# First up product of a mixture-of-experts stage without its second gather, last ranks between its halves, and the list of the 18 later tiles finished ahead of the first gated tile

## The chip, the cores and the metric

The kernel runs on one core of one Trainium2 chip. The metric is the device time of one execution in microseconds; the profiled execution has a span a little below its own time, since the span counts from the first to the last recorded instruction. Engines are named as in the profile: PE is TensorE, PEld its weight load, DVE is VectorE, ACT is ScalarE, POOL is GpSimd, SP is the engine that issues most transfers. A "q" behind an engine's name is its queue (its sequencer).

## The reference

Two layers over x of shape (2, 512, 128), all in float32: cross attention to 77 context rows with 16 heads, then a feed-forward stage of 8 experts of which each row takes the best two. The second layer is what the change touches.

```python
def _L0_ffn_ref(x, Wg, bg, W1, b1, W3, b3, W2, b2):
    logits = x @ Wg + bg
    probs = softmax(logits)
    top_v, top_i = top_k(probs, 2)
    top_v = top_v / (top_v.sum(-1, keepdims=True) + 1e-06)
    combine = einsum('bsk,bske->bse', top_v, one_hot(top_i, 8))
    out = zeros_like(x)
    for e in range(8):
        h = silu(x @ W1[e] + b1[e]) * (x @ W3[e] + b3[e])
        out = out + combine[..., e:e + 1] * (h @ W2[e] + b2[e])
    return out

x = x + _L0_xattn_ref(_layernorm(x), ctx_1024, ...)
x = x + _L0_ffn_ref(_layernorm(x), ...)
```

## The kernel before

The 1024 rows stand in 8 row tiles of 128 (`T = 8`), in three groups: tiles 0 to 3, 4 and 5, 6 and 7. Every row goes to two experts, so there are 2048 pairs of row and expert. They are sorted by expert into `NT = 23` expert tiles of 128 slots, each with the rows of one expert only. The first `FULL = 5` expert tiles are filled from the pairs of groups 0 and 1, before the last row tiles have left the attention; the other 18 take what is left.

The sort is arithmetic on VectorE and TensorE. For a group, `top_two` finds the two experts of each row and writes `sel`; `count_ranks` on TensorE multiplies `sel` by triangular matrices, which gives every pair its rank within its expert; `ranks` and `blocks_of` on VectorE read that out. `first_tiles` and `other_tiles` turn ranks into a list (`hit_1` for 5 tiles, `tile_hit` for 18) that says which pair stands in which tile, `one_hots` writes the permutation `perm` within a tile, and `slot_rows` on TensorE multiplies both (12 or 16 narrow products), so that the row number of every slot comes out in PSUM. VectorE writes them to `idx` (`other_rows` for the 18), and `other_experts` writes the experts' numbers to `eid`.

The expert stage runs over the tiles j = 0 to 22. GpSimd gathers the 128 rows of a tile from memory (`gather`, an indirect transfer), eight tiles ahead, and later scatters the result (`scatter`). TensorE transposes them (`expert_xT`, L1224), ScalarE copies the transpose out of PSUM (L650), TensorE forms the two up products (`up`, L1237: the gate half with W1, the linear half with W3; 16 matrix instructions a tile), ScalarE applies Silu to the gate half (L661), VectorE multiplies (`gated`, L970), TensorE forms the down product (`down`, L1248) and VectorE adds its bias (`bias_down`, L979). The weights of four tiles lie ready (`WR = 4`); SP loads those of tile j when the linear half of tile j - 4 is done. An expert's number is read from `eid` into a register (`value_load`) by each engine that needs it.

Each engine runs its instructions in the order in which they are written. An instruction that waits for a semaphore holds up all behind it on its engine. So the order on TensorE, VectorE and GpSimd around the start of the expert stage is written out by hand, and the change moves things in it. On TensorE it was:

```python
count_ranks(2); expert_xT(0); expert_xT(1)
up(0); expert_xT(2)
up(1); expert_xT(3); slot_rows(T * K, tile_hit, ...); down(0)
up(2); expert_xT(4); down(1)
...
```

On VectorE, behind `other_tiles`: `gated(0)`, `one_hots(2)`, `other_experts`, `gated(1)`, `other_rows`, `bias_down(0)`, `gated(2)`, and so on. On GpSimd: gathers 0 and 1, `rstd_step(6)` (the root of the variance of row tiles 6 and 7, which `top_two(2)` and `normed(2)` need), gathers 2 to 7. Gather 0 waits for the `idx` of the first 5 tiles, gather 5 for that of the 18 and for the last rows in memory.

Of the kernel before, what the change touches and what calls it, by code (L numbers as in the profile page):

```python
# [33 lines left out]
def build(nc, x, ctx_in, w_q, w_kv, w_out, gamma, beta, w_g, b_g, w_1, b_1, w_3, b_3, w_2, b_2, out):  # L34
# [18 lines left out]
    with ctx:  # L53
# [368 lines left out]
        def _(pool):  # L422
# [93 lines left out]

            AHEAD = 8
            for j in range(AHEAD):
                if j == 2:
                    rstd_step(4 + G - 1)  # L520
                gather(j)
            for j in range(NT):
# [152 lines left out]
        def _(dve):  # L675
# [210 lines left out]
            def other_tiles():  # L886

                link(dve.tensor_copy(floor_2[:, PAIRS_1:T * K], floors[:, PAIRS_1:T * K]))
                link(dve.scalar_tensor_tensor(out=padded[:, :], in0=TOTALS[1], scalar=ROUND_128, in1=taken_r[:, :],
                                              op0=ALU.add, op1=ALU.subtract))  # L890
                link(dve.tensor_tensor(low_pad[:, :, 0:E], lower[:, :, :], over_pairs(padded[:, :], E), ALU.mult))
                link(dve.tensor_reduce(base[:, :], low_pad[:, :, :], AX.X, ALU.add))
                link(dve.tensor_tensor(based[:, :, :, :].rearrange("p t k e -> p (t k) e"), masks, over_pairs(base[:, :], T * K), ALU.mult))
                link(dve.tensor_reduce(start_of[:, :, :], based[:, :, :, :], AX.X, ALU.add))
                starts = start_of[:, :, :].rearrange("p t k -> p (t k)")
                link(dve.tensor_tensor(starts, starts, floor_2[:, :], ALU.add))
                link(dve.tensor_tensor(tile_hit[:, :, :],
                                       iota_j[:, FULL:NT].rearrange("p (o j) -> p o j", o=1).broadcast_to([P, T * K, NT - FULL]),
                                       starts.rearrange("p (n o) -> p n o", o=1).broadcast_to([P, T * K, NT - FULL]),
                                       ALU.is_equal))  # L900
                dve.tensor_tensor(tile_hit[:, :, :], tile_hit[:, :, :],
                                  vals.rearrange("p (n o) -> p n o", o=1).broadcast_to([P, T * K, NT - FULL]),
                                  ALU.mult).then_inc(hit_ok, 1)
# [48 lines left out]
            ranks(2)  # L952
            blocks_of(2)
            other_tiles()

            dve.wait_ge(eid_1_ok, 1)
            dve.wait_ge(ld["bias"], 16)
# [16 lines left out]
            def bias_down(j):  # L974

                dve.wait_ge(y_mm, j + 1)
                if j >= YR:
                    dve.wait_ge(y_st[j % YR], 16 * (j // YR))
                dve.tensor_tensor(y_sb[:, j % YR, :], Y_AT[j % 2],  # L979
                                  b2[:, bass.ds(expert[j], 1), :].rearrange("p e d -> p (e d)"), ALU.add).then_inc(y_ok, 1)  # L980
# [10 lines left out]
            for j in range(NT + 1):  # L991
                if j < NT:
                    gated(j)
                if j == 0:
                    one_hots(2)
                if j >= 1 and j != 1:
                    bias_down(j - 1)
                if j == 0:
                    other_experts()
                elif j == 1:  # L1000
                    other_rows()
                    bias_down(0)
                elif j == FULL:
                    dve.tensor_tensor(shifted[:, :, :], top_v[:, :, :], top_v[:, :, 0:1].broadcast_to([P, T, E]),
                                      ALU.subtract).then_inc(shift_ok, 1)

# [11 lines left out]
        def _(pe):  # L1018
# [204 lines left out]
                    pe.wait_ge(xt_ok, j)  # L1223
                pe.transpose(psum[:, 6, 0:P], xg[:, j % GR, :], ident[:, :]).then_inc(xt_mm, 1)  # L1224

            def up(j):

                if j == FULL:
                    pe.wait_ge(eid_ok, 1)
                expert[j] = pe.value_load(eid[0:1, j:j + 1], min_val=0, max_val=E - 1)  # L1230
                pe.wait_ge(xt_ok, j + 1)
                pe.wait_ge(w_ok[j % WR], 32 * (j // WR + 1))
                for a, (freed, done) in enumerate(((silu_ok, gate_mm), (h_ok, lin_mm))):
                    if j >= 2:
                        pe.wait_ge(freed, FC * (j - 1))
                    for c in range(FC):
                        ins = pe.matmul(psum[:, 2 * (j % 2) + a, c * P:(c + 1) * P],  # L1237
                                        w13[:, j % WR, a, c * P:(c + 1) * P],
                                        xt[:, j % XR, :], start=True, stop=True)
                    ins.then_inc(done, 1)  # L1240

            def down(j):

# [74 lines left out]
            slot_rows(FIRST * K, hit_1, FIRST_AT, hit_1_ok, idx_1_mm)  # L1318
            tokens_x2T(2)
            logits(2)  # L1320
            count_ranks(2)
            pe.wait_ge(ld["experts"], 16 * E)
            pe.wait_ge(eid_1_ok, 1)
            expert_xT(0)
            expert_xT(1)
            for j in range(NT + 1):
                if j < NT:
                    up(j)
                if j + 2 < NT:
                    expert_xT(j + 2)  # L1330
                if j == 1:
                    slot_rows(T * K, tile_hit, OTHER_AT, hit_ok, idx_mm)
                if j >= 1:
                    down(j - 1)


# [25 lines left out]
```

## Time and profile before

| what | value |
|---|---|
| three runs, us | 166.34, 167.34, 168.57 (median 167.34) |
| the profiled execution, its own time, us | 168.23 |
| span of the profiled execution, us | 166.2 |
| TensorE busy (matmul) | 135.3 us, 81% of the span |
| VectorE busy | 107.1 us, 64% |
| ScalarE busy | 76.6 us, 46% |
| GpSimd busy | 78.9 us, 47% |
| mean granted clock of TensorE | 0.934 of full |

Times in the profile's views are microseconds from the span's start. A busy share is a mean over stages with different limits: the attention fills the first 70 us or so, the routing of the last rows follows, and the expert stage fills 83 to 152 us. A granted clock of 1.00 is 2.4 GHz, 0.50 is 1.2 GHz.

### The profile page before, as it was taken

The page shows a single profiled execution, that of the slowest core. Times are in us where ns is not written, and L with a number is a line of the kernel's source. Part 1 is how long each engine was busy: PE and PEld are TensorE (multiplying, and loading weights), DVE is VectorE, ACT ScalarE, POOL GpSimd, SP SyncE. Part 2 cuts the span into 40 slices and gives each one's busy share as a digit, 9 for nine tenths or more (in the row PEclk, how much of TensorE's full clock was granted, in tenths as well). Part 3 has the DMA queues.
Part 4 walks back from the last instruction along what each step waited for, and adds up shares of the span by engine and source line. Part 5 has one row for each costly group of instructions (what it writes and reads, how often), then busy time and mean ns, then how long its engine had stood idle before and what let it go on. Part 6 is the DMA issues. An engine that isn't in the chain of part 4 may idle for free.

```text
span 166.2 us, 3861 instructions
## 1 busy us (share of the span) xinstructions
PE 135.3 (81%) x1109; PEld 127.1 (76%) x1109; DVE 107.1 (64%) x345; ACT 76.6 (46%) x210; POOL 78.9 (47%) x98
## 2 busy tenths in 40 slices
PE   6499697889999999864299889999999999994000
PEld 6398586669988999863199789999999999994000
DVE  0685899998899968986758626363636363535074
ACT  3048565875564698600333523545454444444000
POOL 2760300956553685106700677777777744244000
PEclk9999999999999999996569999999999999999555
DMA  4999700011000002338704776877788775300453
GB/s 143 287 319 279 220 2 0 0 63 67 0 2 4 0 0 62 101 111 284 266 21 132 213 243 194 206 262 226 235 248 261 223 264 191 115 16 32 137 165 95
DMA packets 21629, 23.63 MB, mean 142 GB/s; under 512 B 2349, under 2 KB 14473, under 8 KB 21609
## 3 DMA queue, kind: packets, MB, share of 16 engines
q1 hardware_dynamic: 19300, 19.51, 38.3%
q0 software_dynamic: 1472, 3.02, 6.1%
q10 hardware_dynamic: 837, 0.87, 1.5%
q8 instruction: 9, 0.15, 0.4%
q14 instruction: 11, 0.09, 0.2%
HBM read 19.98 MB, written 3.41 MB: 141 GB/s over the span
## 4 chain that ended last, share of the span: by engine, by line
PE 63%; DVE 13%; DMA 10%; ACT 6%; issue 3%; POOL 1%; SPq 1%; ACTq 0%; POOLq 0%; DVEq 0%
PE psum L1237 25%; PE psum L1248 11%; PE psum L1282 8%; PE psum L1264 5%; DMA early<-in_L_xattn_W_kv_dram 4%; DMA g_room<-xf_scratch,idx 3%; PE psum L1021 2%; PE psum L1023 2%; PE psum L1089 2%; PE psum L1022 2%; DMA y_back<-y_scratch 2%; PE psum L1224 2%; DVE prob L747 2%; DVE xn L1014 2%; DVE negmax L742 2%
## 5 line engine op out<-in xcount | busy, mean ns | idle before, releaser
L1237 PE MATMUL psum<-probT,w 128*128 128x128 f32 x368 | 46.5, 281 | 0.7 <-ACT probT L650 0.7
L970 DVE SCALAR_TENSOR_TENSOR probT<-psum,bias_col,prob 128x128 f32<-128x128 f32 x92 | 26.0, 344 | 31.5 <-ACT prob L661 28.9
L1237 PEld LDWEIGHTS psum<-probT,w 128*128 128x128 f32 x368 | 44.4, 197 | 1.3 <-ACT probT L650 0.9
L661 ACT ACTIVATE prob<-psum,bias_col 128x128 f32<-128x128 f32 x92 | 26.3, 369 | 35.6 <-PE psum L1237 33.4
L505 POOL DMA_INDIRECT g_room<-xf_scratch,idx x23 | 22.7, 987 | 23.7 <-DVE idx L917 8.8
L480 POOL TENSOR_TENSOR prob<-prob,rowsum 128x1232 f32<-128x1232 f32 x8 | 18.0, 2251 | 15.3 <-DVE rowsum L738 15.3
L514 POOL DMA_INDIRECT y_scratch<-xnT,out_row x18 | 17.6, 980 | 14.9 <-DVE xnT L979 11.9
L1248 PE MATMUL psum<-w,probT 128*128 x184 | 24.4, 276 | 0.0
L1248 PEld LDWEIGHTS psum<-w,probT 128*128 128x128 f32 x184 | 22.3, 192 | 0.1
L1282 PE MATMUL psum<-vo,probT 128*128 128x128 f32 (+1 forms) x160 | 19.3, 276 | 0.0
L1282 PEld LDWEIGHTS psum<-vo,probT 128*128 128x128 f32 (+1 forms) x160 | 18.5, 192 | 0.0
L601 ACT ACTIVATE probT<-psum 128x512 f32<-128x512 f32 (+1 forms) x24 | 10.9, 493 | 7.5 <-PE psum L1264 7.5
L742 DVE TENSOR_REDUCE negmax<-psum 128x16 f32<-128x1232 f32 x8 | 11.5, 1433 | 2.2 <-PE psum L1023 2.2
L747 DVE TENSOR_TENSOR prob<-psum,negmax 128x1232 f32<-128x1232 f32 x8 | 11.5, 1441 | 0.3
L1264 PE MATMUL psum<-ident,prob 128*128 128x128 f32 x80 | 11.3, 276 | 0.4 <-ACT vo L601 0.4
L735 DVE TENSOR_REDUCE rowsum<-prob 128x16 f32<-128x1232 f32 x8 | 11.3, 1418 | 0.3 <-ACT prob L584 0.3
L584 ACT ACTIVATE prob<-prob 128x1232 f32<-128x1232 f32 x8 | 9.8, 1228 | 2.9 <-DVE prob L747 2.9
L1021 PE MATMUL psum<-g_room,xn_hi 128*128 128x512 f32 (+1 forms) x24 | 9.1, 379 | 1.3 <-issue 1.3
L1264 PEld LDWEIGHTS psum<-ident,prob 128*128 128x128 f32 x80 | 8.7, 140 | 1.2 <-issue 0.6
L1023 PE MATMUL psum<-g_room,xn_hi 128*128 128x512 f32 (+1 forms) x24 | 8.5, 355 | 0.0
L1022 PE MATMUL psum<-g_room,xn_lo 128*128 128x512 f32 (+1 forms) x24 | 8.5, 355 | 0.0
L460 POOL TENSOR_SCALAR rstd<-mv 128x4 f32<-128x4 f32 (+1 forms) x7 | 1.9, 264 | 13.7 <-DVE mv L694 13.7
(162 smaller groups left out, 185.7 us busy)
## 6 DMA issues: line engine op xcount, KB each, us to landing
w<-in_L_ffn_W_dram SPq DMA_DIRECT2D x54, 256.0 KB, 4.8
early<-in_L_xattn_W_kv_dram SPq DMA_DIRECT2D x2, 512.0 KB, 7.5
y_back<-y_scratch SPq DMA_DIRECT2D x4, 256.0 KB, 3.5
early<-in_L_xattn_W_q_dram ACTq DMA_DIRECT2D x1, 512.0 KB, 8.3
early<-in_L_xattn_W_out_dram SPq DMA_DIRECT2D x1, 512.0 KB, 10.1
early<-in_L_ffn_b_dram SPq DMA_DIRECT2D x1, 512.0 KB, 4.3
xf_scratch<-xf SPq DMA_DIRECT2D x2, 256.0 KB, 2.6
xf_scratch<-xf SPq DMA_DIRECT2D x4, 128.0 KB, 2.2
```

The source lines that it names most:

```text
L480: pool.tensor_tensor(prob[:, t % NP_, :].rearrange("p (h m) -> p h m", h=H), prob[:, t % NP_, :].rearrange("p (h m) -> p h m", h=H), rowsu ...
L505: pool.indirect_dma_start(xg[:, j % GR, :], None, xf_dram[:, :], bass.IndirectOffsetOnAxis(ap=idx[:, j:j + 1], axis=0)).then_inc(xg_ok[j % ...
L514: pool.indirect_dma_start(y_dram[:, :], bass.IndirectOffsetOnAxis(ap=rows_of[:, j:j + 1], axis=0), y_sb[:, j % YR, :], None).then_inc(y_st ...
L661: act.activation(silu[:, j % 2, c, :], psum[:, 2 * (j % 2), c * P:(c + 1) * P], ACT.Silu, bias=bias_col[:, 0, bass.ds(expert, 1), c]).then ...
L742: dve.tensor_reduce(negmax[:, t, :], scores(t), AX.X, ALU.max, negate=True).then_inc(s_dve, 1)
L747: dve.tensor_tensor(heads(t), scores(t), negmax[:, t, :].rearrange("p (h o) -> p h o", o=1).broadcast_to([P, H, M]), ALU.add).then_inc(s_s ...
L970: dve.scalar_tensor_tensor(out=hT[:, j % 2, c, :], in0=psum[:, 2 * (j % 2) + 1, c * P:(c + 1) * P], scalar=bias_col[:, 1, bass.ds(expert[j ...
L1021: pe.matmul(dst, w_h, m_h, start=True, stop=False)
L1237: ins = pe.matmul(psum[:, 2 * (j % 2) + a, c * P:(c + 1) * P], w13[:, j % WR, a, c * P:(c + 1) * P], xt[:, j % XR, :], start=True, stop=True)
L1248: ins = pe.matmul(Y_AT[j % 2], hT[:, j % 2, c, :], w2[:, bass.ds(expert[j], 1), c, :].rearrange("p e d -> p (e d)"), start=(c == 0), stop= ...
L1264: ins = pe.transpose(bank[0:rows(c), k * P:(k + 1) * P], prob[:, t % NP_, c * P:c * P + rows(c)], ident[:, :])
L1282: ins = pe.matmul(bank[:, 0:P], probT[0:rows(c), t % 2, c, :], vo[0:rows(c), t // TB, c, :], start=(c == 0), stop=(c == CH - 1))
```

## The change

GpSimd does `rstd_step(6)` ahead of gather 1 instead of ahead of gather 2. TensorE starts `up(0)` after `expert_xT(0)` alone; `count_ranks(2)` goes between the gate half and the linear half of `up(0)`; then come `expert_xT(1)`, `expert_xT(2)` and the `slot_rows` of the 18 tiles, and only then `up(1)`. VectorE does `one_hots(2)` and `other_experts` ahead of `gated(0)` instead of behind it, and `other_rows` behind `gated(0)` instead of behind `gated(1)`.

```diff
             AHEAD = 8
             for j in range(AHEAD):
-                if j == 2:
+                if j == 1:
                     rstd_step(4 + G - 1)
                 gather(j)
...
             other_tiles()
+            one_hots(2)
+            other_experts()
...
                 if j < NT:
                     gated(j)
                 if j == 0:
-                    one_hots(2)
-                if j >= 1 and j != 1:
+                    other_rows()
+                else:
                     bias_down(j - 1)
-                if j == 0:
-                    other_experts()
-                elif j == 1:
-                    other_rows()
-                    bias_down(0)
-                elif j == FULL:
+                if j == FULL:
                     dve.tensor_tensor(shifted[:, :, :], ...)
...
-            def up(j):
+            def up(j, between=None):
...
                     ins.then_inc(done, 1)
+                    if a == 0 and between is not None:
+                        between()
...
             logits(2)
-            count_ranks(2)
             pe.wait_ge(ld["experts"], 16 * E)
             pe.wait_ge(eid_1_ok, 1)
             expert_xT(0)
+            up(0, lambda: count_ranks(2))
             expert_xT(1)
-            for j in range(NT + 1):
+            expert_xT(2)
+            slot_rows(T * K, tile_hit, OTHER_AT, hit_ok, idx_mm)
+            for j in range(1, NT + 1):
                 if j < NT:
                     up(j)
                 if j + 2 < NT:
                     expert_xT(j + 2)
-                if j == 1:
-                    slot_rows(T * K, tile_hit, OTHER_AT, hit_ok, idx_mm)
-                if j >= 1:
-                    down(j - 1)
+                down(j - 1)
```

## Rows read from the trace of the kernel before

**Rows 1.** The chain that ended last, 60 to 167 us: start, length, what.
```profile
77.23 4.69 DMA g_room<-xf_scratch,idx
81.92 0.12 issue
...
83.15 3.47 PE psum L1237 x16
...
102.43 0.89 PE psum L1248 x8
103.32 1.79 PE psum L1237 x16
105.11 0.11 PE psum L1224
```

**Rows 2.** Order of time, 66 to 101 us; in brackets the idle time before, and what ended it.
```profile
72.52 5.56 SPq L387 DMA_DIRECT2D w<-in_L_ffn_W_dram  x8
...
75.69 1.24 POOL L505 DMA_INDIRECT g_room<-xf_scratch,idx  x1 [8.62 <-DVE idx L947]
...
78.21 0.26 POOL L460 TENSOR_SCALAR rstd<-mv 128x2 f32<-128x2 f32 x1
...
79.38 0.16 DVE L778 SCALAR_TENSOR_TENSOR shift<-mv,rstd 128x2 f32<-128x2 f32 x1 [1.49 <-POOL rstd L462]
...
80.77 0.17 DVE L799 TENSOR_TENSOR sel<-mask 128x16 f16<-128x16 f32 x1
...
81.00 0.20 PE L1200 MATMUL psum<-sel,ones 128*128 128x24 f16 x1 [3.27 <-DVE sel L799]
...
81.31 0.19 DVE L806 TENSOR_TENSOR ranked<-mask,psum 128x32 f32<-128x32 f32 x1 [0.36 <-PE psum L1202]
...
82.04 0.45 PE L1224 MATMUL psum<-ident,g_room 128*128 128x128 f32 x1 [0.46 <-DMA g_room<-xf_scratch,idx]
...
84.62 0.46 DVE L901 TENSOR_TENSOR tile_hit<-tile_hit,val 128x288 f16<-128x288 f16 x1
...
86.57 1.95 PE L1237 MATMUL psum<-probT,w 128*128 128x128 f32 x16
...
87.84 0.68 DVE L827 TENSOR_TENSOR perm<-iota_q,q_of 128x512 f16<-128x512 f16 x1
...
88.47 0.55 PE L1213 MATMUL psum<-tile_hit,perm 128*128 128x18 f16 x16
...
89.46 0.16 DVE L912 TENSOR_SCALAR eid<-eid_f 1x18 int32<-1x18 f32 x1
...
90.31 1.13 DVE L970 SCALAR_TENSOR_TENSOR probT<-psum,bias_col,prob 128x128 f32<-128x128 f32 x4 [0.69 <-issue]
...
91.36 0.23 DVE L917 TENSOR_SCALAR idx<-psum,row_base 128x18 uint32<-128x18 f32 x1
...
91.86 0.95 POOL L505 DMA_INDIRECT g_room<-xf_scratch,idx  x1 [8.78 <-DVE idx L917]
...
96.09 0.33 PE L1224 MATMUL psum<-ident,g_room 128*128 128x128 f32 x1 [1.28 <-DVE probT L970]
...
100.37 1.95 PE L1237 MATMUL psum<-probT,w 128*128 128x128 f32 x16
```

**Rows 3.** Gathers (L505): gather 0 alone, then those from 69 to 99 us.
```profile
DMA to landing us min/median/max: 4.5/4.5/4.5
...
DMA to landing us min/median/max: 2.8/4.2/4.7
```

**Rows 4.** L1230 (the expert's number into a register), TensorE's queue, 71 to 100 us.
```profile
L1230 PEldq TENSOR_LOAD <-eid x6: 297/308/612, 82.1 to 98.4; - x6
```

**Rows 5.** Stretches: length, busy time (instructions) by engine, granted clock, transfers' share, GB/s.
```profile
73.20:75.90 2.70, 0.63 (x14) 0.57 (x14) 2.43 (x12) 0.00 (x0) 0.21 (x1) 1.00 0.73 221
76.00:81.00 5.00, 1.17 (x6) 0.93 (x4) 3.06 (x20) 1.26 (x3) 4.08 (x6) 0.50 0.85 308
83.10:86.20 3.10, 3.05 (x14) 3.08 (x15) 1.81 (x6) 0.86 (x4) 0.00 (x0) 0.50 0.10 28
86.20:88.90 2.70, 2.70 (x39) 2.69 (x37) 2.04 (x8) 1.70 (x8) 0.00 (x0) 1.00 0.18 23
```

**Rows 6.** Transfers of the page, by line: transfers, KB each, median us to landing.
```profile
w<-in_L_ffn_W_dram SPq DMA_DIRECT2D x54, 256.0 KB, 4.8
```

## The prediction

> **What bounds the kernel now.** I read the chain of waits first, then the order of time around the diff, then the clock. From about 97 us to 149 us the chain is TensorE without a gap: a tile of the expert stage is 0.89 us of down product, 1.79 us of up product and 0.11 us of transpose, so 2.79 us a tile, repeated unchanged [rows 1]. Nothing in the diff touches that stretch or the tail behind it. So the question is only when TensorE enters it: I take the start of `up(5)`, 100.37 us before [rows 2], as the mark, and whatever moves it moves the end.
>
> Ahead of the mark four things cost time. (1) TensorE stands 3.27 us in front of `count_ranks(2)`, waiting for `sel` [rows 2]. Gather 0 had landed by then: issued at 75.69 [rows 2], 4.5 us to landing [rows 3], so 80.2. (2) It then waits for gather 1 until 82.04 [rows 1, 2], and `up(0)` starts at 83.15. (3) `up(0)` takes 3.47 us against 1.79 us later [rows 1], because the granted clock is 0.50 (1.2 GHz) from about 76 to 86.2 and 1.00 (2.4 GHz) afterwards [rows 5]. (4) Before `expert_xT(5)` it stands 1.28 us, since gather 5 goes out only at 91.86, after `idx` at 91.36 [rows 2]. The change attacks (1), (2) and (4).
>
> **Part 1, `rstd_step(6)` ahead of gather 1.** On POOL the step took from 78.21 to `shift` at 79.38, 1.17 us, and VectorE stood 1.49 us for it [rows 2]. Gather 0's instruction ends at 76.93, so the step now starts there, `shift` falls at 78.1 and `sel` (1.56 us later, 79.38 to 80.94 [rows 2]) is ready at 79.7 instead of 80.94. Gather 1 starts at about 78.2 instead of 77.23; by its own 4.69 us [rows 1] it lands at 82.9. Gathers 2 to 4 keep their places, as the step stood ahead of gather 2 before. `normed(2)` and SP's two stores of the last rows move 1.2 us forward; only gather 5 waits for them, and it waits longer for `idx`. Taken alone the step is worth nothing here, because of part 2: `sel` is now asked for only at 83.1.
>
> **Part 2, `up(0)` without gather 1, ranks between its halves.** `expert_xT(0)` at 80.3 (landing plus 0.12, as after gather 1 [rows 1]). From a transpose to the first product of `up(0)` went 1.11 us (82.04 to 83.15 [rows 1, 2]), in which TensorE's queue reads the expert's number (a register load, 0.61 us the first time [rows 4]) and ScalarE copies; so `up(0)` starts at 81.4, 1.7 us sooner. Its weights were issued from 72.52 [rows 2] and land in a median of 4.8 us [rows 6]; they are there. The gate half costs half of 3.47, 1.73 us, to 83.15; then the four small rank products, which VectorE reads 0.31 us after they begin (81.00 to 81.31 [rows 2]): `ranks(2)` at 83.45, against 81.31 before. **This is the price of the change: the list for the 18 tiles starts 2.1 us later.** The linear half ends at about 85.0, transposes 1 and 2 at about 86.3 with the copy between them (gather 1 landed at 82.9 and is hidden; if it took all of the margin to 85.0 it would begin to cost).
>
> **Part 3, what is now queued behind the list.** `slot_rows` of the 18 tiles stands ahead of `up(1)` on TensorE. `ranks(2)` to the end of `tile_hit` took 81.31 to 85.08, 3.77 us; the permutation, moved in front of `gated(0)`, 0.68 us [rows 2]: 83.45 + 3.77 + 0.68 = 87.9. Until then TensorE can do 12 of the 16 slot products and no more; `up(1)`, whose rows and weights are ready since 86, waits behind them, and all that follows. After 87.9 come the last 4 slot products (a quarter of 0.55 us [rows 2]) and the register load of `up(1)`, which is no longer hidden. No row shows this pair; bounds: 0.2 us (load hidden) and 1.25 us (0.14 plus the 1.11 us in front of `up(0)`). I take 1.05, near the upper one, because the queue holds at the same kind of wait as there, with nothing behind it. So `up(1)` starts at 88.95 instead of 86.57 [rows 2], **2.4 us later**.
>
> On VectorE, `other_experts` now stands ahead of `gated(0)`: 1.1 us (88.52 to 89.62 [rows 2]), then 0.69 us of register load [rows 2]: `gated(0)` at about 89.7, done by 90.9. Who waits: `down(0)`, due at 88.95 + 1.79 + 0.11 = 90.85. Four pieces follow one another at VectorE's pace of 0.28 us, so it hardly stops, but the load for `up(2)` is again behind that wait: 0 to 0.6 us, taken as 0.3. ScalarE's first Silu products come after its second copy, before 88, well ahead of `gated(0)`.
>
> **Part 4, what is given back.** From `up(1)` on no list stands between the tiles. `up(1)` to `up(5)` is then 4 x 2.79 = 11.2 us; before it was 86.57 to 100.37, 13.8 us, with the slot products and the 1.28 us. `other_rows` stands behind `gated(0)` instead of `gated(1)`: `idx` 1.05 us after its start (90.31 to 91.36 [rows 2]), so 90.75, gather 5 0.5 us later at 91.25, landing some 4.2 us after that at 95.5. It is wanted at 96.3 or later: hidden, by 0.8 us; without that cover each late microsecond counts. The weights of tile 5 wait for `up(1)` (90.75 instead of 88.5), land 4.8 us [rows 6] and an issue later, some 96.5, and are wanted at 100.
>
> **Sum.** `up(5)` at 88.95 + 11.16 + 0.3 = 100.4, against 100.37. The wait for gathers is exchanged for a wait for the list, one for one: **0.0 us, from -1.1 to +0.7** by the bounds named.
>
> **The clock.** That sum counts TensorE at 2.4 GHz from `up(1)` on. Before, TensorE was busy 0.63 of the 2.70 us from 73.2 to 75.9, 12 narrow slot products and two transposes in the main, and the clock then fell; it came back at 86.2, at the end of 3.05 us of dense work [rows 5]. The change makes a second thin stretch of the same kind: from 86.3 to 88.95 there are 16 narrow slot products, 0.55 us, and it comes right when the clock has just risen. If it is at 1.2 GHz when `up(1)` begins, that product costs 3.47 instead of 1.79 us [rows 1]: at most 1.7 us more; if it falls or rises inside the product, less. I take 1.2 us.
>
> The Trainium skill (TensorE: Matmul & The Clock Gate, section Loop structure matters more than you think) warns of the same thing: a wait between matmuls lets the engine go cold, and the next ones run slow. Its section on the PE-mode transpose says that transposes do not count as busy work in the same way, so the two of part 2 would not help to hold the clock. By this rule the time is the higher one; by a clock that stays up, the sum stands at 0.0.
>
> **Scale.** The profiled execution took 168.23 us; the three runs have the median 167.34, 0.89 below it. I put each difference on the median. The profiled one lies inside their spread (166.34 to 168.57); if its surplus was a low clock under `up(0)`, which the new order does not shorten, the runs after may lie up to 0.9 us higher.
>
> **Rivals.** *Forecast, 0.45:* the exchange is even and the low clock takes some of `up(1)`: 167.34 + 0.0 + 1.2 = 168.5, from 167.9 to 170.0. *Clock stays up, 0.30:* for it, dense work from 81.4 to 85.0 is as long as what raised it before; against it, the thin stretch: 167.3, from 166.5 to 168.0. *The list is hidden, 0.16:* if the gate half runs at 2.4 GHz it takes 0.87 us less and the list follows at once: 166.5; if the list were ready when the transposes are, `up(1)` could start at 86.9 and `up(5)` at 98.1, 2.3 us earlier: 165.0. For it: the clock's fall at 75.9 came late in a thin stretch and need not come in each run. Against: that list has 1.6 us to make up, and in the trace none of its 14 steps has slack. *Slower, 0.09:* the clock does not come back after `up(1)`, because the wait for `gated(0)` breaks the dense work again. A whole tile at 1.2 GHz costs 2.79 us more, and through `up(2)` it is 2.79 + 1.7 = 4.5: 171.8. It decides from the point where the low clock lasts beyond `down(0)`. Against it: before, the clock rose under one product. *That it does not do what it says* would be gather 0 landing later than 80.2; the rows give 2.8 to 4.7 us for one [rows 3], so 0.2 us at most; it is inside the bounds.
>
> **The numbers.** About 2% (3.3 us) is what a measurement of this kernel can tell from no change. Faster by more needs below 164.0, under even the hidden list's 165.0: 0.04. Slower needs above 170.7: the slow rival, 0.09. Within: 0.87. The range for 8 in 10 goes from 166.2 (most of the hidden list left out) to 170.2 (the forecast's end with the surplus).
>
> **What would show it.** `up(0)` near 81.4, `ranks(2)` near 83.5, TensorE idle some 2 us in front of the slot products, ended by VectorE's `tile_hit` and `perm`; `up(1)` near 89 and its length (1.8 or 3.5 us) with the granted clock; no wait in front of `expert_xT(5)`; `up(5)` at 100 to 102. The prediction is wrong if `slot_rows` finds its list ready, if gather 5 still ends a wait, or if `down(0)` stands for `gated(0)` by more than half a microsecond.

## The result, and the profile after

| | before | changed |
|---|---|---|
| median of 4 runs each, us | 167.95 | 170.64 |
| lowest and highest, us | 166.34, 169.36 | 168.71, 171.53 |
| ratio, 95% interval | | 1.0145 [1.0086, 1.0203] |
| profiled execution: own time, span, us | 168.23, 166.2 | 171.53, 169.5 |
| mean granted clock | 0.934 | 0.912 |

The changed kernel is slower by 1.45%, some 2.4 us. The ratio leaves out executions more than 1.5% above the fastest of their kernel, the profiled one of the changed kernel among them, so it is not the quotient of the two medians. The forecast of 168.5 and its range to 170.2 were too low.

The two profiles first have to be laid over each other. Gather 0 is issued at 75.69 us before [rows 2] and at 76.62 after, although the change does nothing ahead of it; across the profiles below that issue lies anywhere between 74.2 and 76.7. So all times of the stage are given here **from gather 0's issue**. From there to the end of the span went 90.5 us before (166.2 - 75.69) and 92.9 after (169.5 - 76.62): 2.4 us, the same as the timed ratio.

The chain of waits of the changed kernel (start, length, what), as in [rows 1]; in the new line numbers L1221 is the transpose, L1234 the up product, L1247 the down product, L1210 the slot products:

```profile
76.62 4.18 DMA g_room<-xf_scratch,idx
...
82.25 2.05 PE psum L1234 x8
84.42 0.20 DVE ranked L806
...
87.74 0.46 DVE tile_hit L901
88.19 0.61 DVE perm L827
88.86 0.27 PE psum L1210 x4
89.13 0.54 issue
89.66 3.75 PE psum L1234 x16
93.41 0.21 PE psum L1221
93.63 1.71 PE psum L1247 x8
95.33 1.81 PE psum L1234 x16
```

What stands here is the path that the prediction laid out: the gate half of `up(0)` alone, `ranked`, the steps of the list, `perm`, the last four slot products, the register load ("issue"), `up(1)`. New are the two lengths behind it. `up(1)` takes 3.75 us, and `down(0)` 1.71, where a down product takes 0.89 in [rows 1].

The order of time of the same run (start, length, engine, line, operation; in brackets the idle time before it), for the lines that answer to [rows 2]:

```profile
79.11 0.16 DVE L778 SCALAR_TENSOR_TENSOR shift<-mv,rstd 128x2 f32<-128x2 f32 x1 [0.29 <-POOL rstd L462]
...
80.50 0.17 DVE L799 TENSOR_TENSOR sel<-mask 128x16 f16<-128x16 f32 x1
...
84.42 0.19 DVE L806 TENSOR_TENSOR ranked<-mask,psum 128x32 f32<-128x32 f32 x1 [3.75 <-PE psum L1199]
...
88.25 0.88 PE L1210 MATMUL psum<-tile_hit,perm 128*128 128x18 f16 x16 [0.83 <-DVE tile_hit L901]
...
91.97 0.23 DVE L917 TENSOR_SCALAR idx<-psum,row_base 128x18 uint32<-128x18 f32 x1
...
92.47 0.95 POOL L505 DMA_INDIRECT g_room<-xf_scratch,idx  x1 [8.41 <-DVE idx L917]
...
103.56 1.61 PE L1234 MATMUL psum<-probT,w 128*128 128x128 f32 x13
```

VectorE stood 3.75 us in front of `ranked`, for the rank products that now run in the middle of `up(0)`; its `sel` was done at 80.7. The last line is `up(5)`, the mark. It stands 26.94 us behind gather 0, against 24.68 before: 2.26 us of the 2.4. Behind the mark nothing differs by more than 0.1 us.

The stretches (length, busy time with instructions of PE, PEld, DVE, ACT, POOL, then the granted clock, the transfers' share, GB/s), to be read against [rows 5]:

```profile
78.40:82.20 3.80, 0.45 (x1) 0.18 (x1) 1.76 (x14) 1.16 (x3) 2.99 (x4) 0.50 0.97 331
82.20:86.50 4.30, 4.25 (x21) 3.83 (x21) 1.76 (x10) 0.00 (x0) 1.55 (x2) 0.50 0.29 84
86.50:89.60 3.10, 1.22 (x18) 0.76 (x17) 2.86 (x10) 1.59 (x6) 0.00 (x0) 0.50 0.41 135
89.60:95.10 5.50, 5.44 (x25) 5.47 (x26) 2.98 (x13) 1.42 (x5) 2.02 (x3) 0.50 0.11 34
95.50:99.00 3.50, 3.50 (x34) 3.50 (x34) 1.59 (x6) 1.31 (x5) 2.59 (x4) 1.00 0.62 203
```

Here is where the time went. The clock falls to 1.2 GHz ahead of `up(0)`, as before. Then 4.25 us of nearly dense work in `up(0)` do not bring it back, a thin stretch follows (1.22 us busy of 3.10), and `up(1)` and `down(0)` run through at 1.2 GHz. It fell at 78.2 and is back at 2.4 GHz only at 95.3; before, it fell at 75.9 and was back at 86.2. Run 7 below, the same order on TensorE in an execution of 170.67 us, shows the same lengths: `up(1)` 3.75 us, and 5.46 us from `up(1)` to `up(2)`, where this profile has 5.47.

### The profile page after: what moved, and what is told of

The parts are those of the page before. It is cut to its first block, busy times and chain, and to the rows that moved or that the text cites. A ratio compares the mean times of both kernels' runs of the same rounds, so it can differ in the third digit from the quotient of the medians.

```text
span 169.5 us, 3861 instructions
## 1 busy us (share of the span) xinstructions
PE 138.8 (82%) x1109; PEld 130.6 (77%) x1109; DVE 107.1 (63%) x345; ACT 76.6 (45%) x210; POOL 78.8 (47%) x98
## 4 chain that ended last, share of the span: by engine, by line
PE 64%; DVE 15%; DMA 9%; ACT 4%; issue 3%; POOL 1%; SPq 1%; ACTq 0%; POOLq 0%; DVEq 0%
PE psum L1234 25%; PE psum L1247 12%; PE psum L1281 8%; PE psum L1263 5%; DMA early<-in_L_xattn_W_kv_dram 4%; PE psum L1086 3%; DMA g_room<-xf_scratch,idx 2%; PE psum L1018 2%; PE psum L1020 2%; PE psum L1019 2%; DMA y_back<-y_scratch 2%; DVE prob L747 2%; DVE xn L1011 2%; DVE negmax L742 2%; PE psum L1221 2%
## 5 line engine op out<-in xcount | busy, mean ns | idle before, releaser
L1234 PE MATMUL psum<-probT,w 128*128 128x128 f32 x368 | 48.8, 289 | 1.4 <-ACT probT L650 0.9
L1234 PEld LDWEIGHTS psum<-probT,w 128*128 128x128 f32 x368 | 46.4, 204 | 1.7 <-ACT probT L650 1.1
L505 POOL DMA_INDIRECT g_room<-xf_scratch,idx x23 | 22.7, 985 | 23.3 <-DVE idx L947 8.6
L1247 PE MATMUL psum<-w,probT 128*128 x184 | 25.1, 282 | 0.0
L1247 PEld LDWEIGHTS psum<-w,probT 128*128 128x128 f32 x184 | 23.2, 198 | 0.1
L1018 PE MATMUL psum<-g_room,xn_hi 128*128 128x512 f32 (+1 forms) x24 | 9.1, 379 | 1.3 <-issue 1.3
L650 ACT ACTIVATE probT<-psum 128x128 f32<-128x128 f32 x23 | 6.7, 292 | 6.8 <-PE psum L1221 6.8
L1221 PE MATMUL psum<-ident,g_room 128*128 128x128 f32 x23 | 6.9, 301 | 3.2 <-DMA g_room<-xf_scratch,idx 2.7
```

The source lines that it names most:

```text
L505: pool.indirect_dma_start(xg[:, j % GR, :], None, xf_dram[:, :], bass.IndirectOffsetOnAxis(ap=idx[:, j:j + 1], axis=0)).then_inc(xg_ok[j % ...
L1018: pe.matmul(dst, w_h, m_h, start=True, stop=False)
L1247: ins = pe.matmul(Y_AT[j % 2], hT[:, j % 2, c, :], w2[:, bass.ds(expert[j], 1), c, :].rearrange("p e d -> p (e d)"), start=(c == 0), stop= ...
```

## The experiments

What is to be told apart: is the loss (a) the clock, (b) the wait for the list in front of `up(1)`, or (c) something else in the new order, such as the early `rstd_step`? Two tools serve for it. The first is filling: products of the identity with itself, put where TensorE stands idle and written to a place of PSUM that is written anew before it is read, to hold the clock up (`hold(n)` is n products, each two matrix instructions; ten took 2.48 us in run 1). The second moves `slot_rows` and the ranks. No kernel leaves any of the computation out. "Mark" is the start of `up(5)` in the profiled run, from gather 0. One execution of each run was profiled, and the granted clock differs between executions, so marks and times agree only loosely. In the changed orders `up(0)` starts anywhere from 5.46 to 6.05 us, as gather 0 lands, so a mark alone is good to about half a microsecond.

**1. The changed kernel with filling ahead of `up(0)` and five products in front of the last `slot_rows`.**

```diff
+            def hold(n):
+                for k in range(n):
+                    pe.matmul(psum[:, 2, 0:P], ident[:, :], ident[:, :], start=True, stop=True)
...
+            hold(5)
             slot_rows(FIRST * K, hit_1, FIRST_AT, hit_1_ok, idx_1_mm)
+            hold(2)
             tokens_x2T(2)
+            hold(2)
             logits(2)
+            hold(10)
...
+            hold(5)
             slot_rows(T * K, tile_hit, OTHER_AT, hit_ok, idx_mm)
```

> The changed order, with extra products of the identity on TensorE in its idle stretches (5 before the first slot products, 2 and 2 around the transposes of the last rows, 10 behind the logits, 5 before the slot products of the 18 tiles); they write a free PSUM bank and nothing reads them. Theory A (the order is an even exchange and the loss is the low clock through up(1) and down(0)): the granted clock stays at 1.00, the gate half takes 0.9 us instead of 2.05, the list starts 1 us sooner, up(1) takes 1.8 us; up(5) starts some 23.3 us after gather 0 is issued instead of 26.9, so about 3.5 us below the changed kernel, 1.2 us below the kernel before. Theory B (the loss is the wait for the list in front of up(1), whatever the clock): the time stays within 1 us of the changed kernel, about 2 us over the kernel before.

Measured: 166.86 us, ratio to before 0.9969 [0.9933, 1.0005], against 1.0145 without the filling. Mark 24.91, 2.03 less. Products that compute nothing take away some 1.8% of the time: the clock it is, in the main. But one part was not cured. The stretches of this run, and `up(1)` from its order of time:

```profile
83.00:84.10 1.10, 1.10 (x11) 0.93 (x9) 0.96 (x5) 0.93 (x4) 0.00 (x0) 1.00 0.16 28
84.10:86.40 2.30, 0.75 (x18) 0.57 (x17) 2.16 (x7) 0.38 (x2) 0.00 (x0) 1.00 0.60 216
86.90:90.00 3.10, 3.10 (x17) 3.10 (x16) 1.59 (x7) 1.14 (x4) 0.77 (x1) 0.50 0.01 3
```
```profile
86.39 3.57 PE L1234 MATMUL psum<-probT,w 128*128 128x128 f32 x16 [0.52 <-issue]
```

`up(0)` ran at full clock (1.13 and 1.14 us a half). After the wait for the list (0.75 us busy of 2.30) the clock fell, 0.2 us into `up(1)` (at 86.6). So the clock can be lost in this wait also where it stood at 2.4 GHz.

**2. The kernel before with the same filling ahead of `up(0)`** (`hold(12)` behind `logits(2)`).

```diff
             logits(2)
+            hold(12)
             count_ranks(2)
```

> The order before, with the same extra products of the identity (5, 2, 2, and 12 behind the logits). Theory A: up(0) takes 1.8 instead of 3.5 us and the mark comes 1.5 us sooner: 1 to 1.7 us below the kernel before, and equal to the changed order with held clock within 0.5 us. Theory B: gather 5 ends the wait in front of up(4) anyway, so no change from the kernel before (within 0.5 us), and the changed order with held clock stays 2 us above it.

Measured: 167.16 us, 0.9965 [0.9917, 1.0013], mark 24.53 (before 24.68). In the profiled run the filling ended at 79.7, the clock fell at about 82.9, just as `up(0)` began, and `up(0)` took 3.65 us. The filling was too short, so this run doesn't tell what the order before costs at full clock; run 9 does.

**3. The slot products behind `up(1)`, as before, everything else changed.**

```diff
-            slot_rows(T * K, tile_hit, OTHER_AT, hit_ok, idx_mm)
             for j in range(1, NT + 1):
                 if j < NT:
                     up(j)
                 if j + 2 < NT:
                     expert_xT(j + 2)
+                if j == 1:
+                    slot_rows(T * K, tile_hit, OTHER_AT, hit_ok, idx_mm)
                 down(j - 1)
```

> The change with one part undone: the slot products of the 18 tiles stand behind up(1) and its transpose again, as before; all else as changed. Theory A: TensorE goes from up(0) through two transposes to up(1) with hardly a gap, so the clock is back before up(1) ends; down(0) waits for gated(0) behind the list; up(5) some 24.5 us after gather 0: about 2.4 us below the changed kernel, level with the kernel before (within 0.7 us). Theory B: the wait for the list moves to down(0) and costs the same: within 0.7 us of the changed kernel.

Measured: 168.47 us, 1.0059 [1.0013, 1.0105], mark 25.29, 1.65 less than changed. `up(1)` now waits for no list and starts at 11.49 instead of 13.04, yet it takes 3.73 us. The wait is worth 1.5 us at `up(1)`, and taking it away alone doesn't bring the clock back in time.

**4. Run 3 with the filling of run 1 ahead of `up(0)`, and `other_experts` moved behind `other_rows`.**

```diff
             one_hots(2)
-            other_experts()
...
                 if j == 0:
                     other_rows()
+                    other_experts()
```

> A candidate: the change with the slot products behind up(1), other_experts behind gated(0) and other_rows on VectorE, and the extra products of the identity ahead of up(0) as in the first run. Theory A: clock at 1.00 throughout; list ready about 87, hidden by up(1); up(5) some 21.5 us after gather 0, 3 us below the kernel before (164.5 to 166). Theory B: the wait for the list is the cost and it is hidden here, so also below the kernel before, but no lower than the run without extra products.

Measured: 165.0 us, 0.987 [0.9755, 0.9985], mark 22.48. With no wait for the list and the clock up, `up(1)` starts at 9.17 and takes 2.02 us. Both causes taken away give a kernel faster than before.

**5. Run 1 with the wait for the list filled as well.**

```diff
-            hold(5)
+            hold(8)
             slot_rows(T * K, tile_hit, OTHER_AT, hit_ok, idx_mm)
+            hold(2)
...
+                    if k == 0 and t == FIRST:
+                        hold(2)
                     if k == 0 and t in (0, FIRST):
```

> The changed order with the identity products ahead of up(0) as before (5, 2, 2, 10), and more of them in the second thin stretch: 8 ahead of the slot products of the 18 tiles, 2 between the first 12 and the last 4, 2 behind them. Theory A (the low clock through up(1) is the whole loss): up(1) takes 1.8 instead of 3.6 us, up(5) stands some 23.3 us behind the issue of gather 0; about 1.5 us below the first held run, so 165.3. Theory B (the wait for the list is the loss): no change from the first held run, 166.9.

Measured: 167.43 us, 0.9969 [0.9932, 1.0005], as run 1. Mark 24.24. The stretch in front of `up(1)` and `up(1)` itself, then both up products in the order of time:

```profile
85.70:89.10 3.40, 3.19 (x40) 2.99 (x40) 3.12 (x11) 1.31 (x5) 0.00 (x0) 1.00 0.44 154
89.10:91.10 2.00, 2.00 (x20) 2.00 (x20) 0.94 (x5) 0.76 (x3) 0.00 (x0) 1.00 0.03 12
```
```profile
89.15 1.95 PE L1236 MATMUL psum<-probT,w 128*128 128x128 f32 x16
...
92.41 2.02 PE L1236 MATMUL psum<-probT,w 128*128 128x128 f32 x16 [0.30 <-issue]
```

The clock is now 1.00 throughout and `up(1)` takes 1.95 us, 1.6 less than in run 1. At the mark only 0.67 of it is left and in the time nothing: `up(1)` starts 0.49 later than in run 1 (0.41 of it already at `up(0)`), and from `up(1)` to `up(2)` go 3.26 us instead of 2.79, because `down(0)` now comes before `gated(0)` is done and the register load for `up(2)` stands behind that wait. This is the bubble of the prediction, 0.47 us (it took 0.3); at 1.2 GHz the slow `up(1)` had hidden it.

**6. Run 1 with transposes as the filling**, two for each product.

```diff
-                    pe.matmul(psum[:, 2, 0:P], ident[:, :], ident[:, :], start=True, stop=True)
+                    pe.transpose(psum[:, 2, 0:P], ident[:, :], ident[:, :])
+                    pe.transpose(psum[:, 2, 0:P], ident[:, :], ident[:, :])
```

> The first held run with each extra product replaced by two transposes of the identity, equally long on TensorE. If transposes hold the clock as products do: same as the first held run (166.9, clock 1.00 ahead of up(0)). If they don't count: the clock falls near 78 us as in the changed kernel and the time is about that of the changed kernel (170).

Measured: 167.84 us, 0.9999 [0.9962, 1.0036], mark 23.97. Stretches of its profile:

```profile
77.50:82.00 4.50, 3.09 (x25) 2.69 (x25) 2.43 (x16) 1.16 (x3) 3.57 (x6) 1.00 1.00 341
...
88.60:90.60 2.00, 1.95 (x17) 1.98 (x18) 0.94 (x5) 0.68 (x3) 0.00 (x0) 1.00 0.02 9
```

Here the clock stays at 1.00 with transposes: from 77.5 through `up(1)`, where the changed kernel's stood at 0.50 from 78.4. Two transposes fill as long as one product: ahead of `up(0)` 2.37 us against 2.48 in run 1, in front of the slot products 1.25 against 1.28. That run 1 lost the clock in this wait and run 6 didn't, with all but the same busy time, need not be due to the kind of filling; one profile of each can't tell. The time is no better than run 1's.

**7. `rstd_step` back in its old place, the rest changed.**

```diff
-                if j == 1:
+                if j == 2:
                     rstd_step(4 + G - 1)
```

> The change with one part undone: rstd_step(6) behind gather 1 again. Both theories: sel comes 1.2 us later, still 2 us before count_ranks(2) asks for it, so the same time as the changed kernel within 0.5 us (ratio to before 1.012 to 1.018). If it is lower, the late gather 1 did cost; if higher, sel was asked for sooner than the trace shows.

Measured: 170.84 us, 1.0164 [1.0089, 1.0239], mark 27.40; changed 1.0145 and 26.94. Part 1 makes no difference that can be told in this order, as predicted. The stretches of this run show something else:

```profile
81.00:84.00 3.00, 2.93 (x16) 2.89 (x17) 0.65 (x4) 0.00 (x0) 1.22 (x2) 0.50 0.49 133
84.30:87.60 3.30, 1.31 (x18) 0.81 (x17) 3.02 (x11) 1.59 (x6) 0.00 (x0) 1.00 0.31 91
88.40:93.90 5.50, 5.44 (x25) 5.47 (x26) 3.01 (x13) 1.42 (x5) 2.00 (x3) 0.50 0.06 15
```

In this run `up(0)` did raise the clock (its second half took 1.67 us instead of 2.06), and it was lost again: it fell at about 87.7, before `up(1)`, which took 3.75 us as ever. So the low `up(1)` doesn't hang on whether `up(0)` raises the clock.

**8. Run 4 without its filling** (the list late, the clock left alone).

```diff
-            hold(10)
```

(and the other `hold` lines likewise)

> The candidate without extra products: slot products behind up(1), other_experts behind gated(0) and other_rows. Theory A: up(0) and up(1) follow each other closely, the clock is low under up(0) and most of up(1) as in the third run, but VectorE reaches gated(0) 1.1 us sooner: 1 us below the third run, so 167.5, level with the kernel before; the candidate with held clock stays 2.5 us below it. Theory B: the list is hidden, so level with the candidate with held clock (165).

Measured: 168.82 us, 1.0022 [0.9966, 1.0078], mark 25.94; 167.5 had been expected. Without filling `up(1)` starts at 11.32 and takes 3.76 us. The filling ahead of `up(0)` is worth 3.46 us at the mark in this order (25.94 - 22.48), and some 2.5 us by the two ratios.

**9. The kernel before at full clock**: run 2 with filling around its transposes.

```diff
+            hold(2)
             expert_xT(0)
+            hold(3)
             expert_xT(1)
+            hold(3)
             for j in range(NT + 1):
```

> The order before with identity products in all its idle stretches up to up(0) (5, 2, 2, 12, and 2, 3, 3 around the first two transposes), so that up(0) itself runs at 2.4 GHz. Theory A (at equal clock the two orders are an even exchange): up(5) some 24.2 us behind the issue of gather 0, as in the changed order at full clock (24.24), 0.4 us below the kernel before. Theory C (the even sum had the low clock under up(0) in it, and at equal clock the changed order is the slower one): up(0) takes 1.8 instead of 3.5 us and everything behind it, idx and gather 5 too, comes 1.5 us sooner: up(5) at 23.2, 1.5 us below the kernel before and 1 us below the changed order at full clock.

Measured: 165.93 us, 0.99 [0.9859, 0.9941], mark 23.38. From its order of time, `up(0)`, `up(1)` and the transpose of tile 5:

```profile
82.54 2.02 PE L1237 MATMUL psum<-probT,w 128*128 128x128 f32 x16
84.50 1.95 PE L1237 MATMUL psum<-probT,w 128*128 128x128 f32 x16
...
93.98 0.33 PE L1224 MATMUL psum<-ident,g_room 128*128 128x128 f32 x1 [1.06 <-DVE probT L970]
```

So the kernel before paid for the clock too, 1.3 us at the mark, and at full clock it still has the wait for gather 5 (issued at 90.01, landed 3.9 us later), 1.06 us, that the change removes.

**10. The changed kernel with only the wait for the list filled.**

```diff
+            hold(3)
             slot_rows(T * K, tile_hit, OTHER_AT, hit_ok, idx_mm)
```

> The changed order with identity products in its second thin stretch alone (3 ahead of the slot products of the 18 tiles, 1.3 us at 1.2 GHz); the clock has fallen near 78 us as without them. Theory A: with them the work from up(0) on is dense enough for the clock to come back about the start of up(1): up(1) 1.8 to 2.5 us instead of 3.75, 1.5 us below the changed kernel (ratio to before about 1.005). If the first thin stretch (74 to 81 us) is what counts: no change from the changed kernel (1.0145).

Measured: 168.59 us, 1.008 [1.0035, 1.0126], mark 24.65, 2.29 less than changed. Its stretches, then the filling (L1260) and `up(1)`:

```profile
81.00:85.20 4.20, 3.99 (x21) 3.52 (x20) 1.96 (x11) 0.18 (x1) 1.39 (x2) 0.50 0.34 97
85.40:88.10 2.70, 1.69 (x23) 1.37 (x24) 2.49 (x9) 1.30 (x5) 0.00 (x0) 1.00 0.54 171
```
```profile
85.58 0.83 PE L1260 MATMUL psum<-ident 128*128 128x128 f32 x6
88.10 2.02 PE L1234 MATMUL psum<-probT,w 128*128 128x128 f32 x16 [0.52 <-issue]
```

`up(0)` is at 1.2 GHz throughout (2.05 and 2.06 us a half). The clock is back at 85.4, before the first product of the filling at 85.58, so the filling didn't raise it. What differs from run 7, where the clock also came back with `up(0)`, is that it lasts: it stays at 1.00 through the wait, and `up(1)` takes 2.02 us. So this profile shows the changed order with the clock lost under `up(0)` alone. That the three products kept it is likely from run 7, but rests on one profile of each. The time moves by less than the mark (0.65% or 1.1 us), and the mean clocks of its ten executions go from 0.909 to 0.948, so the clock may not be caught in each.

**11. Part 1 alone in the kernel before.**

```diff
             for j in range(AHEAD):
-                if j == 2:
+                if j == 1:
                     rstd_step(4 + G - 1)
```

> The kernel before with rstd_step(6) ahead of gather 1 and nothing else. Both theories: sel comes 1.2 us sooner, but gather 1 lands 1 us later and up(0) still waits for it: up(0) at 84.1 instead of 83.15; list 1.2 us sooner, gated(0) and idx 1 us later; 0.5 to 1.0 us over the kernel before (ratio 1.003 to 1.006), within what can be told from no change.

Measured: 167.67 us, 0.9992 [0.9947, 1.0036]. `up(0)` starts 0.56 us later (8.02 instead of 7.46), since it still waits for gather 1; the mark is at 24.40 against 24.68. A loss of 0.3 to 0.6% was expected; there is none that can be told.

**12. Run 4 with `other_experts` later still**, behind `gated(1)` and the `bias_down` of tile 0.

```diff
                     other_rows()
-                    other_experts()
                 else:
                     bias_down(j - 1)
+                if j == 1:
+                    other_experts()
```

> The best candidate so far with other_experts moved once more, behind gated(1) and the bias of tile 0, so that down(1) no longer waits for it. All theories: up(2) to up(3) 2.8 instead of 3.45 us, up(5) some 21.8 us behind gather 0, 0.6 us below the candidate: 164.4, ratio to before 0.983; unless the weights of tile 5, which then go out 1 us later, hold up(5).

Measured: 164.98 us, 0.9864 [0.9772, 0.9955], mark 22.37 against 22.48. From `up(2)` to `up(3)` go 2.86 us instead of 3.45, the 0.6 expected. The mark shows only 0.1 of it, since `up(0)` started 0.47 later (6.05 against 5.58); the times of four executions each don't tell the two apart.

**13. The changed kernel with the ranks ahead of `up(0)`.**

```diff
+            count_ranks(2)
             pe.wait_ge(ld["experts"], 16 * E)
             pe.wait_ge(eid_1_ok, 1)
             expert_xT(0)
-            up(0, lambda: count_ranks(2))
+            up(0)
```

> The changed order with one part undone: count_ranks(2) stands ahead of expert_xT(0) and up(0) again, not between the halves. Theory D (the price at equal clock is the late start of the list, and the thin stretch that it makes lets the clock down): sel is there 4.1 us behind the issue of gather 0, before gather 0 lands (4.2 to 4.7), so the four rank products cost nothing; the list starts at 4.4 instead of 7.8 and is done when TensorE comes to it (10.6); no thin stretch behind up(0); up(1) at about 11.4, up(5) at 22.9: 1.8 us below the kernel before, 4 us below the changed kernel (165.8). If the loss were in the other moves (slot products ahead of up(1), other_experts ahead of gated(0)): as the changed kernel.

Measured: 167.53 us, 0.9927 [0.987, 0.9983]; by the medians of all executions, 167.53 against 168.08, it is 0.997. TensorE in the order of time:

```profile
80.45 0.20 PE L1197 MATMUL psum<-sel,ones 128*128 128x24 f16 x1 [2.51 <-DVE sel L799]
...
81.00 0.45 PE L1221 MATMUL psum<-ident,g_room 128*128 128x128 f32 x1 [0.29 <-DMA g_room<-xf_scratch,idx]
...
82.18 3.75 PE L1234 MATMUL psum<-probT,w 128*128 128x128 f32 x16 [0.73 <-ACT probT L650]
...
86.85 0.62 PE L1210 MATMUL psum<-tile_hit,perm 128*128 128x18 f16 x16
...
87.61 3.75 PE L1234 MATMUL psum<-probT,w 128*128 128x128 f32 x16
```

The rank products run at 80.45, while gather 0 is still landing: they cost TensorE nothing. `sel` is done 4.04 us behind gather 0's issue, where the kernel before had it at 5.25 [rows 2], later than gather 0 lands; so part 1 should earn its place here, though no run leaves it out of this order. The permutation starts at 8.10 instead of 11.49 and the slot products no longer wait for it (nothing stands in brackets). What failed is the clock again: `up(1)` takes 3.75 us and the mark comes at 24.44, not at the 22.9 expected. The stretch that holds what stands between the two up products, two transposes with a copy between them and the slot products:

```profile
86.00:88.00 2.00, 1.41 (x20) 1.18 (x20) 0.53 (x4) 1.20 (x5) 0.00 (x0) 0.50 0.20 31
```

TensorE is busy for 1.41 us of the 2.00.

**14. Run 13 with the filling ahead of `up(0)`** (`hold(9)` behind `logits(2)`).

```diff
             logits(2)
+            hold(9)
             count_ranks(2)
```

> The same with identity products ahead of it (5, 2, 2, 9), so that up(0) runs at 2.4 GHz too: up(0) takes 1.8 us, the slot products wait a little for perm (done at 8.8), up(1) at 9.8, up(5) at 21.2 behind gather 0: 3.4 us below the kernel before (164.2), the lowest of all.

Measured: 164.37 us, 0.9829 [0.9759, 0.9899], the lowest of all, though the intervals of runs 4 and 12 overlap it; mark 21.41. Both up products at 2.4 GHz, and no wait for `perm`:

```profile
78.66 0.19 PE L1197 MATMUL psum<-sel,ones 128*128 128x24 f16 x1 [0.41 <-DVE sel L799]
...
80.00 2.02 PE L1234 MATMUL psum<-probT,w 128*128 128x128 f32 x16 [0.69 <-ACT probT L650]
...
84.16 2.02 PE L1234 MATMUL psum<-probT,w 128*128 128x128 f32 x16 [0.51 <-issue]
```

**15 and 16. Runs 5 and 9 once more, side by side**, for the two orders at full clock.

```diff
+                    if k == 0 and t == FIRST:
+                        hold(2)
...
+            hold(3)
             expert_xT(1)
+            hold(3)
```

(the edits are those of run 5 and of run 9, in full)

> The changed order at full clock once more, beside the next run on the same chip. Theory C: 0.86 us above the order before at full clock (the traces' 24.24 against 23.38). Theory A: equal to it.

> The order before at full clock once more, beside the run above. Theory C: 0.86 us below it, 1.3 us below the kernel before. Theory A: equal to the run above.

Measured: the changed order 167.39 us, 0.997 [0.993, 1.001], marks 23.84 (run 5: 24.24); the order before 166.22 us, 0.9923 [0.9879, 0.9967], marks 23.52 (run 9: 23.38). With means of two marks, the changed order comes 0.6 us later at equal clock (24.04 against 23.45); the intervals of the times just overlap.

## Why the prediction was wrong

**Right: the path and almost all of its times.** From gather 0, forecast and measured: `up(0)` 5.71 and 5.63; `ranks(2)` 7.76 and 7.80; the permutation done 12.2 and 12.18; `up(1)` 13.26 and 13.04; gather 5 issued 15.56 and 15.85, and hidden, with no wait at `expert_xT(5)`. Only the idle time in front of the slot products was 0.83 us, not "some 2 us". "The wait for gathers is exchanged for a wait for the list, one for one" holds in the profile. Run 10 is the very case that the sum counted, `up(0)` at 1.2 GHz and all from `up(1)` on at 2.4: its mark is 24.65 against 24.68, and 0.0 had been forecast. The bubble of `down(0)` didn't show in the changed kernel, since VectorE was done while `up(1)` was slow; run 5 shows it at 0.47 us, where 0.3 was taken.

**The step that failed is the clock term**: "at most 1.7 us more; if it falls or rises inside the product, less. I take 1.2 us." Its mechanism was right, its size not. It counted one product at 1.2 GHz. Measured were `up(1)`, the transpose behind it and `down(0)`, all at 1.2 GHz until 95.3 us: `up(1)` to `up(2)` took 5.47 us, and a tile at 2.4 GHz takes 2.79 [rows 1], so 2.68 us. Part of it only covers the bubble; net, the changed kernel's mark is 2.29 us behind that of run 10 (26.94 - 24.65) and 2.26 behind before. The bound of 1.7 left room for one product at 1.2 GHz, as the clock rose under one `up(0)` before [rows 5]. But the dense work is broken in front of `up(1)`: run 7 shows that a clock back in `up(0)` can be lost in the wait, run 1 that even a clock held up until then can be lost there, and runs 5, 6 and 10 that with filling in the wait `up(1)` ran at 2.4 GHz. The rival that it lasts "beyond `down(0)`" was priced at 4.5 us and had its cause elsewhere (`gated(0)`); the truth lay between it and the forecast, and no case stood there. The miss of 168.5 by 2.1 us has a second, smaller part: the base. The four runs before have the median 167.95 where the forecast took 167.34, 0.6 us; between the two medians lie 2.7 us where it took 1.2, the other 1.5.

**A second thing the sum concealed** is that before, too, was slowed by the clock. The forecast's 0.0 compared an order with `up(0)` at 1.2 GHz to one with `up(0)` at 1.2 GHz. Freed of it, before gains 24.68 - 23.45 = 1.23 us at the mark, the changed order 26.94 - 24.04 = 2.90, and 0.6 us are left for the orders themselves. The times say the same: 0.77% (1.3 us) from before to run 16, 1.75% (2.9 us) from changed to run 15. So of the 2.3 us lost, 1.7 are the clock and 0.6 the order, as far as means of two profiles go. The fillings stand on TensorE too: in runs 9 and 16 `up(0)` starts 0.25 and 0.36 us later than in the kernel before, so the 0.6 isn't free of them.

**The Trainium skill** (TensorE: Matmul & The Clock Gate, section Loop structure matters more than you think) gave the direction: a wait between products made the next ones slow, `up(1)` 3.75 us against 1.95 to 2.02 in runs 5, 10 and 14. What the same page says of the PE-mode transpose (Part 4), that it doesn't count as busy work in the same way, run 6 doesn't bear out as far as keeping the clock goes: filled with transposes, it kept the granted clock at 1.00. No run shows whether transposes would raise it.

**The wait for the list is not the whole of the clock's story.** Runs 3, 8 and 13 have no such wait ahead of `up(1)` and still run it at 1.2 GHz, 3.73 to 3.76 us. What they share with the changed kernel is that `expert_xT(1)` and `expert_xT(2)` stand between the first two up products; before, one transpose did, and `up(1)` took 1.95 us [rows 2]. No run moved `expert_xT(1)` alone, so this is argued from the busy share (1.41 of 2.00 us in run 13), not shown. Nor is the return of the clock the same in each profile: with `up(0)` at 1.2 GHz in the changed order, it came back in or just behind `up(0)` in runs 7 and 10, and not in the changed kernel and runs 3, 8 and 13. On TensorE run 10 and the changed kernel do the same up to there, so that return is not the filling's doing, and what a filling in the wait can gain depends on it.

**What the change did right** appears when the list starts early. Run 13 differs from the changed kernel by the place of four small rank products, and goes from 1.0145 to 0.9927 (by medians, from 1.016 to 0.997). "This is the price of the change: the list for the 18 tiles starts 2.1 us later" was right. That the price need not be paid the prediction did not see: with part 1, `sel` is ready before gather 0 has landed, and the ranks fit ahead of `up(0)` for nothing. "Taken alone the step is worth nothing here" held for part 1 in the changed order and in the one before (runs 7 and 11); in the order of run 13 the times of `sel` speak for it, untested.

**Open.** What activity brings the clock back isn't settled: 3.05 us of dense work did before [rows 5], 4.25 us did not after. Why gather 0's issue varies between profiles isn't either: from 75.14 to 76.74 in those without filling, and among those with the same filling ahead of it run 1 has it at 74.34 and run 5 at 76.61. And the 0.6 us between the orders at full clock has 0.3 to 0.9 as its ends. That spread is the start of `up(0)`, 5.60 and 6.00 in the changed order, 7.71 and 7.82 in the one before; from there to the mark the runs repeat, 18.24 us twice and 15.67 and 15.70.

## What to carry to other kernels

When a change puts a wait in front of dense work, price every instruction until the granted clock is back, not the first alone, and price in the same way what the kernel before already loses to the clock. Start the longest chain first: small products that open a chain on another engine belong ahead of a large product whose data are still on their way. If the order can't close a gap, a few products in it, which nobody reads, are a cheap test of whether the clock is the cause; look then at when the clock rose or fell against when they ran.

## What the hardware showed that was not expected

- `up(0)` at 1.2 GHz, 4.25 us busy of 4.30, did not raise the clock, though 3.05 us busy of 3.10 did before [rows 5]; in run 7 it rose under 2.93 us busy of 3.00.
- The clock can fall in the product after the gap: in run 1 it was 1.00 through the thin stretch and fell at 86.6, 0.2 us into `up(1)`, which took 3.57 us.
- With transposes of the identity in its idle stretches, TensorE kept the clock at 1.00 (run 6).
- A register load that isn't hidden costs TensorE 0.5 us between the last slot product and `up(1)` (0.54 after, where the load itself took 0.31 from 88.9 on; 0.52 in run 1, 0.51 in run 14).
